# Rows scattered to expert slots in the attention stages, and tiles loaded by ScalarE, in a two-layer attention and expert kernel

## The reference

```python
x = x + attn_a(layernorm(x))      # 16 heads of 64, causal, slopes on the distance
x = x + ffn(layernorm(x))
x = x + attn_b(layernorm(x))      # 8 heads of 128, rotary positions, causal
x = x + ffn(layernorm(x))

# ffn, for every row h of the 4096 (normalized again by its mean square, times norm_w)
logits = h @ gate_w.T + gate_b                     # 8 experts
vals, idx = top_k(logits, 2); wts = softmax(vals)
t1 = h @ mlp1_w[e].T + mlp1_b[e]                   # 256 -> 512, for the 2 chosen experts
glu, lin = min(t1[::2], 7), clip(t1[1::2], -7, 7)
y_e = (glu * sigmoid(1.702 * glu) * (lin + 1)) @ mlp2_w[e].T + mlp2_b[e]
h_out = h + sum of wts[j] * y_e[j]
```

## Time and profile before

| | |
|---|---|
| three runs | 2229.5, 2229.8, 2231.53 us; median 2229.8 |
| profiled execution | 2217.43 us, span 2215.5 |
| PE busy | 2052.4 us (93%) |
| DVE busy | 1568.7 us (71%) |
| ACT busy | 1442.5 us (65%) |
| POOL busy | 1308.6 us (59%) |
| indirect DMAs of GpSimd | 142 gathers (144.8 us), 142 scatters (144.5 us), 128 id puts (128.7 us) |
| bytes moved | 134.42 MB |

### The profile page before, as it was taken

How to read it: one execution, slowest core, us unless ns; L and a number is a source line. 1 busy time by engine, 2 the same in 40 slices (tenths; PEclk the granted TensorE clock), 3 DMA queues, 4 the chain that set the end, 5 groups by cost and what they waited for, 6 DMA issues and landing times.

```text
span 2215.5 us, 38087 instructions
## 1 busy us (share of the span) xinstructions
PE 2052.4 (93%) x11638; PEld 1629.8 (74%) x11638; DVE 1568.7 (71%) x4433; ACT 1442.5 (65%) x3763; POOL 1308.6 (59%) x1466
## 2 busy tenths in 40 slices
PE   7899999999999999797998999999999999888895
PEld 6677777777777776575776787887878877676774
DVE  7867676868686868465666778677786776656567
ACT  5768787878686867433444868767777676633344
POOL 4665464646464655566665556667576565556563
PEclk9999999999999999999999999999999999999998
DMA  4330020101010000523341101011010001533347
GB/s 147 133 111 30 1 30 1 30 1 30 1 30 1 20 1 22 176 94 77 103 146 58 39 30 39 12 38 46 13 39 30 1 20 58 169 84 97 98 127 246
DMA packets 59932, 134.42 MB, mean 61 GB/s; under 512 B 12948, under 2 KB 31156, under 8 KB 58840
## 3 DMA queue, kind: packets, MB, share of 16 engines
q1 hardware_dynamic: 42008, 94.68, 12.8%
q0 software_dynamic: 17728, 37.32, 6.5%
HBM read 83.59 MB, written 48.40 MB: 60 GB/s over the span
## 4 chain that ended last, share of the span: by engine, by line
PE 68%; DVE 13%; ACT 6%; issue 5%; another core or an unknown queue 4%; POOL 1%; DMA 1%; SPq 0%; ACTq 0%; DVEq 0%; POOLq 0%
PE bank L639 5%; PE bank L657 5%; PE bank L2327 5%; PE bank L679 5%; PE bank L1568 4%; PE bank L624 3%; PE bank L625 3%; PE bank L1553 2%; PE bank L2301 2%; PE bank L2303 2%; PE bank L2302 2%; PE bank L1469 2%; PE bank L570 2%; PE bank L572 2%
## 5 line engine op out<-in xcount | busy, mean ns | idle before, releaser
L1178 POOL TENSOR_TENSOR P<-P,rc 128x128 f32<-128x128 f32 (+3 forms) x512 | 354.4, 723 | 342.0 <-DVE rc L984 341.8
L976 DVE CUSTOM_DVE_ANT_0 P<-bank,tab 128x512 f32<-128x512 f32 (+3 forms) x512 | 241.3, 485 | 105.6 <-PE bank L625 102.2
L807 ACT ACTIVATE P<-P,mn 128x128 f32<-128x128 f32 (+3 forms) x512 | 281.7, 552 | 34.2 <-DVE mn L976 30.7
L818 ACT COPY PT<-bank 128x512 f32<-128x512 f32 (+1 forms) x384 | 194.0, 516 | 107.3 <-PE bank L639 98.1
L2058 POOL TENSOR_TENSOR rf<-rp 128x512 f32<-128x512 f32 x128 | 163.9, 1281 | 134.9 <-DVE rp L1891 134.1
L2069 POOL TENSOR_TENSOR q<-rf,q 128x512 fp32r<-128x512 f32 x128 | 163.1, 1296 | 117.5 <-ACT q L1693 117.2
L639 PE MATMUL bank<-cst,P 128*128 128x128 f32 x1280 | 207.2, 276 | 15.4 <-POOL P L1178 9.6
L2600 POOL DMA_INDIRECT yD<-Yf,place x142 | 144.5, 1018 | 123.5 <-ACT Yf L2405 90.3
L624 PE MATMUL bank<-q 128*128 128x512 f32 (+3 forms) x512 | 185.2, 373 | 21.3 <-DVE mn L976 11.6
L329 POOL DMA_INDIRECT Gf<-hD,idx x142 | 144.8, 1020 | 74.4 <-issue 37.1
L639 PEld LDWEIGHTS bank<-cst,P 128*128 128x128 f32 x1280 | 153.0, 141 | 43.0 <-POOL P L1178 12.9
(11 more groups left out here) (272 smaller groups left out, 6037.2 us busy)
## 6 DMA issues: line engine op xcount, KB each, us to landing
hD<-hh SPq DMA_DIRECT2D x16, 512.0 KB
yg<-yD SPq DMA_DIRECT2D x14, 512.0 KB, 4.6
X<-in_x SPq DMA_DIRECT2D x8, 512.0 KB, 4.6
stage<-in_w SPq DMA_DIRECT2D x8, 512.0 KB, 3.7
w1hD<-W1A SPq DMA_DIRECT2D x8, 512.0 KB
w1lD<-stage SPq DMA_DIRECT2D x8, 512.0 KB
rD<-xn SPq DMA_DIRECT2D x8, 512.0 KB
W1lf<-w1lD SPq DMA_DIRECT2D x1, 4096.0 KB
```

The source lines that it names most:

```text
L807: i = e.activation(ps, ps, ACT.Exp, bias=mn[:, pb, t:t + 1], scale=-1.0, accum_out=rs[:, pb, t:t + 1])
L818: e.copy(PT[:, h % 2, PTO[cs[0]]:PTO[cs[0]] + w], bank[4 + n % 2][:, 0:w]).then_inc(q.a_pt, 1)
L976: e.tensor_tensor_reduce(out=P[:, pb, OFF[t]:OFF[t] + w], in0=score(h, t), in1=tab[:, 512 - w:512], scale=-SLOPES[h % 16], scalar=3e38, op ...
L1178: i = e.tensor_tensor(ps, ps, rc[:, h % 3, t:t + 1].broadcast_to([128, w]), ALU.mult)
```

## The change

**Rows go to slots.** GpSimd's new `put_rows` (L322 after the change) scatters the rows `hh` of a sentence to `hS[slot]` in HBM by eight indirect DMAs of 128 rows, beside the eight of ids. A tile is then 128 rows that follow one another in `hS`. SyncE's store to `hD`, the 142 gathers and `idx` go; `places` has three pieces instead of six. VectorE computes one more row of numbers, `rtab`: where each tile starts.

**Loads.** `load(a)` reads the tile's start into a register and issues a plain DMA of 128 rows. SyncE issues it for tiles 0 to 3, ScalarE for 4 to 70, each right behind `x_high(a - 4)`.

**Fill.** So that slots without a row hold finite numbers, SyncE writes constants over the slots of a sentence ahead of its rows: `fill`, one DMA from HBM to HBM of 4 MB a sentence, 8 a stage. In attention A it stands behind the store of `xn` and the fetch of X of each sentence.

**Places.** In attention A the rows of sentence bt − 1 are put in units 6 and 7 of sentence bt and 0 and 1 of the next, the ids in units 2 to 5 of the next (for the last sentence four in unit 2 and four in 3). In attention B: rows in 6, 7 and 0, ids in 1 to 4. In the experts' stages one id put stands in each of tiles 0 to 7, and 16 puts (8 of ids, 8 of rows) in tiles 16 to 27. In attention B `dI` is computed at step 47 instead of 53. `pick` of the second list moves from tile 31 to 33. SyncE's list in the experts' stages is written anew with the same waits, the rows of `xr` and the weights of `stage` now in one order by tiles. `store_r`, `fetch_rows` and others are the old functions under a new split.

```diff
+        def put_rows(e, q, ph, bt, n, hh):
+            s = NB * ph + bt
+            t, j = divmod(n, 2)
+            if n == 0:
+                e.wait_ge(r_sl, s + 1)
+                e.wait_ge(d_z, 32 + 16 * (s + 1))
+            e.indirect_dma_start(hS[ph], bass.IndirectOffsetOnAxis(ap=dI[:, t, j:j + 1], axis=0), hh[:, t],
+                                 None).then_inc(q.d_h, 16)
+
+        def fill(e, ph, s):
+            e.wait_ge(d_z, 32 + 16 * (NB * ph + s))
+            block = hS[ph].rearrange("(k s p r) d -> s p k (r d)", k=E, s=NB, p=128)[s]
+            src = T["tab"][1][:, 1:3].rearrange("p a b -> p (a b)").rearrange("p (a n) -> p a n", a=1)
+            e.dma_start(block, src.broadcast_to([128, E, 1024])).then_inc(d_z, 16)
+
-        def gather(e, ph, q, a):
+        def load(e, ph, q, a):
             if a == 0:
-                e.wait_ge(r_ls, 4 * ph + 2)
-                e.wait_ge(q.d_h, 16 * K1)
+                e.wait_ge(r_sel, 2 * ph + 1)
+                e.wait_ge(q.d_h, 128 * K1)
                 e.wait_ge(q.p_xs, NB - 2)
...
             if a > 3:
                 e.wait_ge(f_x, NS * ph + a - 3)
-            rows = hD[ph][0:K1 * N] if a < L1 else hD[ph]
-            e.indirect_dma_start(Gs[ph][:, a % 4], None, rows, bass.IndirectOffsetOnAxis(
-                ap=idx[:, a:a + 1], axis=0)).then_inc(d_g[a % 4], 16)
+            row = e.value_load(rtab[0:1, a:a + 1], min_val=0, max_val=E * 32 - 1)
+            rows = hS[ph].rearrange("(n p) d -> p n d", p=128)[:, bass.ds(row, 1)]
+            e.dma_start(Gs[ph][:, a % 4], rows.rearrange("p n d -> p (n d)")).then_inc(d_g[a % 4], 16)
...
 # attention A, GpSimd, unit p of sentence bt
-                        if p == 7 and bt and bt + 1 < NB:
-                            for n in range(4 if bt == K1 else 2):
-                                put_ids(e, 0, bt - 1, n)
-                        if bt == K1 + 1 and p == 0:
-                            for n in range(4, 8):
+                        if bt and p > 5:
+                            for n in (2 * p - 12, 2 * p - 11):
+                                put_rows(e, q, 0, bt - 1, n, hh)
+                        elif bt > 1 and p < 2:
+                            for n in (2 * p + 4, 2 * p + 5):
+                                put_rows(e, q, 0, bt - 2, n, hh)
+                        elif bt == K1 + 1 and p < 4:
+                            for n in range(4 * p - 8, 4 * p - 4):
                                 put_ids(e, 0, bt - 2, n)
-                        elif 1 < bt <= K1 and p < 3:
-                            for n in (2 * p + 2, 2 * p + 3):
+                        elif 1 < bt <= K1 and p < 6:
+                            for n in (2 * p - 4, 2 * p - 3):
                                 put_ids(e, 0, bt - 2, n)
...
 # experts, ScalarE
                         e.copy(XTh[:, k], src).then_inc(a_fx, 1)
+                        if a + 4 < NS:
+                            load(e, ph, q, a + 4)
...
 # experts, GpSimd
-                    for n in range(4):
-                        put_ids(e, ph, BL - 1, n)
-                    gather(e, ph, q, 4)
-                    gather(e, ph, q, 5)
-                    gather(e, ph, q, 6)
-                    for n in range(4, 8):
-                        put_ids(e, ph, BL - 1, n)
                     for a in range(NS):
-                        if a + 7 < NS:
-                            gather(e, ph, q, a + 7)
-                        if 16 <= a < 28 and a % 3 != 0:
-                            put_ids(e, ph, BL, (a - 16) - (a - 16 + 1) // 3)
+                        if a < 8:
+                            put(BL - 1, a)
+                        elif 16 <= a < 28:
+                            for n in range(4 * (a - 16) // 3, 4 * (a - 15) // 3):
+                                put(BL, n)
```

More of the change, by code:

```diff
@@ L1297, in sync @@
                             fetch_x(bt + 2)
+                        if bt and bt + 1 < NB:
+                            fill(e, 0, bt + 1)
                         if bt == 0:
@@ L1314, in sync @@
                             e.dma_start(w1lD[0:1, :, 0:512], first[1]).then_inc(d_w1o, 16)
+                            fill(e, 0, 0)
+                            fill(e, 0, 1)
+                    for a in range(4):
+                        load(e, 0, q, a)
                     e.wait_ge(d_w1o, 32 * E + 48)
@@ L2595, in gpsimd, with put @@
                 def gpsimd(e, late, begin=None):
-                    deviation, mean_square, residual = late
+                    deviation, mean_square, residual, hh = late
+                    def put(bt, n):
+                        if n < 8:
+                            put_ids(e, ph, bt, n)
+                        else:
+                            put_rows(e, q, ph, bt, n - 8, hh)
                     def scatter(a):
+                        if a in (0, L1):
+                            e.wait_ge(r_ls, 2 * ph + (2 if a else 1))
                         e.wait_ge(a_y, T0 + a + 1)
@@ L2664, in sync @@
                         store_r(BL - 1)
+                        for a in range(4):
+                            load(e, ph, q, a)
                         e.wait_ge(q.a_q, 2 * NU)
@@ new lines, in sync @@
+                    for a in range(4, NS):
+                        if a == 16:
+                            store_r(BL)
+                        if a == 37:
+                            fetch_ids(e, ph, 1)
+                        if not last:
+                            if a == 19:
+                                e.wait_ge(q.m_lg, 2 * NB)
+                                stage_in(0)
+                                stage_in(1)
+                            elif a % 4 == 0 and 28 <= a <= 64:
+                                stage_in((a - 20) // 4)
+                            if a == 64:
+                                begin[4](e)
+                            elif a == 65:
+                                begin[5](e)
+                        else:
+                            if a in (19, 22, 25, 28):
+                                fetch_r((a - 19) // 3)
+                            elif a in (45, 49, 53, 57):
+                                fetch_r((a - 29) // 4)
+                            if a == 65:
+                                for k in range(4):
+                                    e.wait_ge(d_y[k], 16 * ph * ((NS + 3 - k) // 4) + 16 * ((LA + 3 - k) // 4))
+                                e.wait_ge(q.h_in, NB)
+                                fetch_rows(0, 1)
+                                fetch_rows(0, 0)
+                            elif 65 < a < NS - 1:
+                                fetch_rows((a - 64) // 2, 1 - a % 2)
@@ L2765, in _ @@
             late = first[4](e)
-            second[4](e, late)
+            second[4](e, late, begin)
             late = third[4](e)
```

177 lines of the change are left out of this document (78 added, 99 removed).

## The result

The changed kernel takes 2280.36 us (median of 4 runs, 2278.0 to 2286.77), the kernel before 2230.06 (4 runs, 2229.5 to 2231.53): a ratio of 1.0229, 95% interval 1.0207 to 1.0251. Forecast were 2202 and a range of 2150 to 2236. The profiled execution took 2281.76 us, span 2278.9, which is 63.4 more than the span before. The runs' medians differ by less, 50.3 us: the profiled execution of the kernel before took 2217.43 us, 12.4 under its median, that of the changed kernel 1.4 over its own.

The account below looks back on a forecast made before the run. The prediction took TensorE as the bound, except in the experts' stages, which lose time in holes behind GpSimd's DMA runs. −63 + 6 + 20 + 2.5 + 7 = −27.5 us, from 2229.8 to 2202; range 2150 to 2236.

Parts of the forecast that it names:

- −51 of −63 us: Experts' stages: taking the gathers off GpSimd breaks its runs of software DMAs, gaining 26 us in the first, 25 in the second.
- the 3 us left for it: Experts' tiles 0 to 7: a scatter and an id put each stay as dense as before, leaving 3 us of loss.
- Rival D: Experts' stages: runs of software DMAs don't make the holes, so the 63 us gain stays out; 2265 us, chance 0.05.
- the wait at dI: +20, bounds 0 and 32: Attention A, sentences 2 to 6: VectorE's slot numbers wait for the last ids to land, 4 us each, +20 us.
- Rival B: Attention A: puts land behind the fill, so VectorE waits about 13 us for each of 5 sentences; 2247 us, chance 0.10.
- ScalarE's load, +6: Experts' stages: ScalarE's loads take 1.1 us a tile, just hidden at TensorE's pace; +6 us over both stages.
- Rival C: Experts' stages: ScalarE's load binds, at 1.8 us the loop is 3.5 a tile; 2257 us, chance 0.06.
- Attention B, +7: Attention B: first two ids exceed the slack, 1.2 us for 5 sentences, +6, and +1 for the last one's three rows.
- The starts, −8 and −4: Starts of the experts' stages: a shorter run of GpSimd DMAs gains 8 us in the first, 4 in the second.
- A's end, +2.5: Attention A, last sentence: two row puts in unit 6 push the last scaling; +2.5 us.

Follow-up runs that it names:

- e4: The changed kernel with 16 more indirect DMAs on GpSimd in tiles 44 to 59 of experts 0; 2289.66 us.
- e3: The kernel before with the 16 fills of 4 MB added, which nothing reads; 2230.65 us beside 2229.96, ratio 1.0001.
- b_again: The kernel before, unchanged, run with a trace of its own on another chip; 2148.45 us.
- e1: The changed kernel with each fill issued only when the ids put beside it have landed; 2239.59 us beside 2229.96, ratio 1.0055.
- e9: e6 with the ids of attention B put in units 1, 2, 3 and 5 instead of 1 to 4; 2162.95 us beside 2147.91.
- e10: e11 with the fills of both attention stages waiting until the next slot numbers are written; 2187.04 us beside 2220.82, ratio 0.9838.
- e11: e6 with the experts' puts spread over more tiles and the id places of e9; 2164.76 us beside 2220.82, ratio 0.9738.
- e12: e11 with the fill waiting for the next slot numbers in attention A alone; 2146.77 us beside 2148.48, ratio 0.9993.
- e6: The changed kernel with two dI buffers and SyncE's fetch of ids and loads moved behind weights ahead of experts 1; 2167.60 us beside 2145.88.

## Why the prediction was wrong

**Its largest gain rested on a rule that the runs limit.** The step "while GpSimd's software DMAs follow one another without a pause, signals between the other engines arrive late" was read off and gave −51 of −63 us. The reading had a flaw: the hole at 1040.53 starts 24.5 us after the last of the twelve, with more scatters, gathers and puts between. On the first chip the rule holds in part: e4 made 6 us of holes with 16 more puts, and the stages gained 18.5 + 22.7 = 41.2 in the two traces (52 against e3's stages) where 51 were forecast. The loss in tiles 0 to 7 was more than the 3 us left for it: down(1) to down(16) stayed at 52.6, where 15 undisturbed tiles take 42. On the chip of b_again there is next to nothing to gain (1.1 and 3.6 us), because most of the holes aren't there in the unchanged kernel. Rival D took all gain away. That is what happens there, but not on the chip that the forecast was for.

**The step that failed was the wait at dI: +20, bounds 0 and 32.** The waits took 63.7 us, and the five sentences 71 us more: 51 of the 78 us between forecast and result. The place, the cause and the unit were right; the size was not. The landing by itself was taken from the earlier trace rows as 8.7 us, and that was right: without a fill ahead it took 5.1 to 11.5 us in e1, 8.0 in the mean. e1's waits of 29.1 us in all, 5.8 a sentence, aren't far from the 4 that the prediction took. The other 35 us are the fill's, which the prediction priced within the 4 us, from the best rate in the trace: 10 or 20 us for 4 MB. It takes 17.8 by itself and 39 with ids among it. Rival B had this mechanism with 13 us a sentence (measured: 12.7) and 2247 in all, at a chance of 0.10; the 33 us between 2247 and the measured time are in the other steps of this section. It deserved the first place: SyncE's order put the fill ahead of the ids in every sentence, and nothing in the rows excluded the upper bound. By the rule of the Trainium skill ("DMA: Bandwidth & Descriptors", the software path) the landing was to take about 2 us; e1 measured 5.1 to 11.5 without a fill ahead, so here the measurement decides against it.

**ScalarE's load, +6.** It costs nothing. One tile of the changed kernel, to hold against the earlier trace rows:

```profile
1183.29 0.38 ACT L2400 CAST XThf<-bank 128x256 fp32r<-128x256 f32 x1
1183.92 0.35 ACTq L347 DMA_DIRECT2D Gf<-hS  x1
1184.84 0.37 ACT L2416 COPY ATf<-bank 128x256 f32<-128x256 f32 x1 [1.17 <-issue]
```

From the end of the copy, 1183.67, to the end of the issue, 1184.27, it is 0.6 us where 1.1 was taken, and it lies in the 1.17 us in which ScalarE idled anyway; down(43) to down(70) keeps a pace of 2.79 us a tile. Rival C falls.

**Attention B, +7.** It was +19. The 1.2 us for the first pair of ids is there (unit 4 takes 16.2 instead of 15.0), though unit 7 gives 1.0 back (19.4 instead of 20.4). Missing were the cast (e9), 11 us over sentences 3 to 5, and sentence 2 (+10.3 in all). There the fill goes out at 1499.49 and an id put at 1500.07, and all engines stand still; TensorE's next instruction in the changed kernel's timeline:

```profile
1509.01 3.36 PE L1586 MATMUL bank<-PT,V 128*128 128x512 f32 x4 [8.91 <-issue]
```

e10, with the fill behind the ids, hasn't this pause; e11 and e12, with the fill there, have one of 3.4 and 1.7 us.

**The starts, −8 and −4.** Experts 0 began 1.3 us earlier, experts 1 4.8 us later. "SyncE, where nothing waits that is near the end" was wrong: the fetch of ids and the loads stood ahead of experts 1's weights (e6). A's end, +2.5, was +7.1. The unit with the rows costs 2.3 of it, as forecast (9.8 instead of 7.5). The rest lies in units 1 and 3 of the last sentence (14.4 and 15.2 instead of 11.9 and 12.5), near the two groups of four ids; that these are the cause wasn't tested.

## What to carry to other kernels

Before pricing what a transfer costs, list what is issued behind it in the next 40 us and who waits for that. Here 67 MB of copies were free alone, and cost 35 us ahead of small puts that an engine waits for; a second buffer for 8 numbers a row took the wait away. A gain that rests on waits of unknown origin in one trace needs a second trace on another chip: here the same unchanged kernel had them on one and not on the other. And compare the profiled execution with the median before its stretches are used as prices: that of the kernel before was 12 us fast, and e3 shows 5 to 6 us more in each experts' stage.

## What the runs showed of the hardware that was not expected

- The unchanged kernel takes 2230, 2221 or 2146 to 2148 us by the group of runs, each within 0.3% of its median but for the profiled execution before (2217.43). Between the traces at 2215.5 and 2145.4 most of the difference lies in the experts' stages (237 against 205 us each), where GpSimd's indirect DMAs are dense. Why was not found.
- Indirect puts of 128 numbers of 4 bytes land late: 12.89 us after the start of the last of eight in the changed kernel's chain at 1969.31, 11.5 us in sentence 2 of e1, with no fill ahead, 8.7 us in the earlier trace rows.
- A copy of 4 MB from HBM to HBM runs at 322 GB/s alone; with id puts among it the rate fell from 233 to 132, 70 and 93.
- A cast of 128x32 on VectorE took 7.2 us, until the end of ten GpSimd operations, where two indirect DMAs stood right ahead of them, and 0.3 us where they didn't (e9) or where 0.28 us lay between.
